# Causal attention with the normalisation on ScalarE, one root step, a single-precision projection, and the experts' loop written out

## The chip, the cores and the metric

The kernel runs on one core of a Trainium2 chip. The metric is the device time of one execution in microseconds (us). The core has engines that run side by side and wait for each other through semaphores: TensorE (PE, with its weight loads as PEld), VectorE (DVE), ScalarE (ACT), GpSimd (POOL), and SyncE (SP), which issues transfers. Each engine works through its own list of instructions in order, so an instruction that waits holds up everything behind it on that engine.

## The reference, cut to what matters

The network has two layers on x of shape 32 x 128 x 128 (32 sequences of 128 tokens, 128 features). The change lies in the last sub-layer, where a causal attention is followed by a mixture of experts:

```python
ln1_out = _layernorm(hidden_states, ln1_weight, ln1_bias)      # input is itself a normalised x
qkv = jnp.einsum('sbh,oh->sbo', ln1_out, qkv_weight)           # 16 query heads, 4 key/value heads of 8
scores = jnp.einsum('sbhd,tbhd->bhst', q, k) * scale
scores = jnp.where(causal, scores, jnp.finfo(scores.dtype).min)
probs = jax.nn.softmax(scores, axis=-1)
attn = jnp.einsum('bhst,tbhd->sbhd', probs, v).reshape(S, B, H)
hidden_after_attn = hidden_states + jnp.einsum('sbh,oh->sbo', attn, proj_weight)
ln2_out = _layernorm(hidden_after_attn, ln2_weight, ln2_bias)
gate = softmax(router logits); top 2 of 8 experts weigh gelu(ln2_out @ w1) @ w2
return hidden_after_attn + moe_out
```

The sequence axis of this attention is the batch axis of x: 128 independent causal attentions over 32 positions each. The input of the attention is normalised twice in a row: once as x's layer norm (the hidden state that the residual adds to), and once more by `ln1`. With variance v the first root is (v + eps)^-1/2. The second one acts on values whose variance is v / (v + eps), and the two together come to (v(1 + eps) + eps^2)^-1/2.

## The kernel before

The program has four parts one after the other: `layer0` and `attention1` (not touched), `attention2` (causal attention, about 561 to 744 us) and `experts1` (744 to 978 us).

`attention2` handles the 128 attentions as 32 steps ("quads") of 4, and 4 quads make a chunk: chunk n covers quads 4n to 4n + 3, and there are 8 chunks. Each engine runs a Python-unrolled function `step(q)` with n, k = q // 4, q % 4. Nothing but the order of these functions and their semaphores sets the order of the work. Around quad q:

- PE (`step` at L1425): transposes the row maxima of quad q (L1429), computes scores K.Q into bank TB (L1432, after the exponential of quad q - 1 has read it), then the scores Q.K of quad q + 1 into bank SB (L1441, L1443). SB also held the transposed maxima, so L1441 waits until ScalarE has copied them (`mT_ready`, the tile `mc`, L1216). Then come products of the next chunk's projections (`slot`: two at k = 0, two at k = 1, one at k = 2; lines 95 to 97), `widen` at k = 1 (L1422), `turn` at k = 3 (L1375, which transposes the normalised input of chunk n + 2), the subtraction of the maxima (L1455), the values (L1398) and the weighted sums of quad q - 1 (L1406, L1411).
- ACT (`step` at L1211): `mc` of quad q (L1216), the `slot` copies (L1201), at k = 1 and 2 two spreads of K (L1208), the exponential of quad q (L1226), at k = 0 a copy of the sums (L1231), and at k = 3 the copy of the transposed input (`high`, L1195) and the high half of the attention's output (L1236, f16 tile AT[0]).
- DVE (`step` at L1303): the maxima of quad q + 1 (L1307 to L1313), the `slot` rests (L1295, L1299), the masked values (L1320), at k = 1 `normalise(n + 2)` (L1281, four instructions of 128x128) and Af (L1344), at k = 2 the statistics (L1269, L1274), at k = 3 the low half of the transposed input (L1287) and the low half of the attention's output (L1347, f16 tile AT[1]).
- POOL (`step` at L1151): at k = 0 the sum Xq + Yq of chunk n + 3 (L1157), at k = 2 `prep(n + 3)`, a chain of seven dependent small instructions with two powers (L1137 to L1143), at k = 3 `hidden(n + 3)` (L1147).

Before quad 0 the same functions run the first chunks in from q = -12.

`experts1` goes over 8 groups of 4 sequences, 16 half-experts p per group. Per p, PE computes three f16 products of 128x512 (lines 95 to 97 with `w1`) and four f32 products of 128x128 (L1734, each recorded as two). At p = 0 it also computes the attention's projection of the next group as four split products of three f16 matmuls each (L1703, recorded at lines 95 to 97 as wp,AT), at p = 6 it transposes and at p = 9 it computes the router's logits. `over_groups` writes the steps for g = -1, 0 and 7 out and runs g = 1 to 6 in a hardware loop whose semaphore targets are computed in registers.

Of the kernel before, what the change touches and what calls it, by code (L numbers as in the profile page):

```python
# [12 lines left out]
F16 = mybir.dt.float16  # L13
# [7 lines left out]
G = B // GB  # L21
# [996 lines left out]
def attention2(nc, d, bank, keep, H, AT, wp):  # L1018
# [9 lines left out]
    with ExitStack() as ctx:  # L1028
# [10 lines left out]
        half = sb("half2", [128, 4])  # L1039
# [12 lines left out]
        rs = [sb(f"rs2_{i}", [128, 6, 4]) for i in range(2)]  # L1052
# [16 lines left out]
            s_psum s_max m_hi m_lo mT_psum mT_ready t_psum p_ready v_psum v_ready pv_done o_sb dd_inv dd_hi dd_lo r_psum at_f at_hi at_lo""")  # L1069
# [17 lines left out]
        with nc.Block() as block:  # L1087
            @block.gpsimd
            def _(pool):
# [40 lines left out]
                def prep(n):  # L1130
                    r, v = rs[n % 2], mv[n % 2][:, :, 1]

                    def link(ins, i):
                        ins.then_inc(s["root"], 1)
                        pool.wait_ge(s["root"], 7 * n + i)
                    pool.wait_ge(s["mv_ready"], n + 1)
                    link(pool.tensor_scalar(r[:, 0, :], v, 1.0, LN_EPS, ALU.mult, ALU.add), 1)  # L1137
                    link(pool.tensor_tensor(r[:, 1, :], r[:, 0, :], half[:], ALU.pow), 2)
                    link(pool.tensor_tensor(r[:, 2, :], r[:, 1, :], r[:, 1, :], ALU.mult), 3)
                    link(pool.tensor_tensor(r[:, 2, :], r[:, 2, :], v, ALU.mult), 4)  # L1140
                    link(pool.tensor_scalar(r[:, 3, :], r[:, 2, :], 1.0, LN_EPS, ALU.mult, ALU.add), 5)
                    link(pool.tensor_tensor(r[:, 4, :], r[:, 3, :], half[:], ALU.pow), 6)
                    link(pool.tensor_tensor(r[:, 5, :], r[:, 4, :], r[:, 1, :], ALU.mult), 7)  # L1143

                def hidden(n):
                    for k in range(4):
                        last = pool.tensor_scalar(H[:, 4 * n + k, :], Xq[:, 4 * n + k, :], mv[n % 2][:, k, 0:1],  # L1147
                                                  rs[n % 2][:, 1, k:k + 1], ALU.subtract, ALU.mult)
                    last.then_inc(s["h_ready"], 1)
# [17 lines left out]
            def _(act):  # L1167
# [18 lines left out]
                act.activation(wp[0][:], bank[1][:, 0:128], ACT.Copy).then_inc(s["hi"], 1)  # L1186
# [4 lines left out]
                act.wait_ge(s["zeros"], 1)  # L1191

# [18 lines left out]
                def step(q):  # L1211
# [16 lines left out]
                    if k == 0 and chunk(n - 1):  # L1228
                        act.wait_ge(s["pv_done"], q)
                        after(act, s["at_f"], n - 1)  # L1230
                        act.activation(Of[:], O[:], ACT.Copy).then_inc(s["o_sb"], 1)  # L1231
                    if k == 3 and chunk(n + 2):
                        high(n + 2)
                    if k == 3 and chunk(n - 1):
                        act.wait_ge(s["at_f"], n)
                        act.activation(tok(AT[0], n - 1), Af[:], ACT.Identity, bias=bv[:]).then_inc(s["at_hi"], 1)  # L1236
# [4 lines left out]
            def _(dve):  # L1241
# [4 lines left out]
                dve.tensor_tensor(wp[1][:], bank[1][:, 0:128], wp[0][:], ALU.subtract)  # L1246
# [29 lines left out]

                def normalise(n):
                    dve.wait_ge(s["root"], 7 * (n + 1))
                    after(dve, s["xT_psum"], n)
                    for k in range(4):  # L1280
                        last = dve.tensor_scalar(xn[:, k, :], Xq[:, 4 * n + k, :], mv[n % 2][:, k, 0:1],  # L1281
                                                 rs[n % 2][:, 5, k:k + 1], ALU.subtract, ALU.mult)
                    last.then_inc(s["xn_ready"], 1)
# [19 lines left out]
                def step(q):  # L1303
# [21 lines left out]
                    if k == 1 and chunk(n + 2):  # L1325
                        normalise(n + 2)
# [13 lines left out]
                    if k == 1 and chunk(n - 1):  # L1340
                        dve.wait_ge(s["r_psum"], n)
                        dve.wait_ge(s["o_sb"], n)
                        after(dve, s["at_lo"], n - 1)
# [129 lines left out]
def experts1(nc, d, bank, keep, X3, H, AT, wp, out):  # L1473
# [5 lines left out]
    with ExitStack() as ctx:  # L1479
# [43 lines left out]
        with nc.Block() as block:  # L1523
# [12 lines left out]
            def _(pool):  # L1536
# [17 lines left out]
                over_groups(pool, step, -1, G - 1)  # L1554

            @block.scalar
            def _(act):
# [26 lines left out]
                over_groups(act, step, -1, G - 1)  # L1584

            @block.vector
            def _(dve):
# [98 lines left out]
                over_groups(dve, step, -1, G - 1)  # L1686
# [4 lines left out]
            def _(pe):  # L1691
# [58 lines left out]
                over_groups(pe, step, -1, G - 1)  # L1750
# [4 lines left out]
def build(nc, d, out):  # L1755
    with ExitStack() as ctx:
# [22 lines left out]
        AT = [room.sb(f"AT{i}", [C, S * B], F16) for i in range(2)]  # L1779
        wp = [room.sb(f"wp{i}", [C, C], F16) for i in range(2)]  # L1780
# [20 lines left out]
```

## Time and profile before

| | us |
|---|---|
| median of 3 runs | 976.86 (973.74 to 979.70) |
| the profiled execution | 979.73 |
| its span, first to last instruction | 978.0 |
| PE busy | 783.1 (80%) |
| DVE busy | 689.6 (71%) |
| ACT busy | 429.1 (44%) |
| POOL busy | 220.6 (23%) |

The profile is of one execution. 1.73 us of its time lie outside the span. Busy shares are averages over four parts with different limits, so below they are read by stretch. A timeline row reads: start, duration, engine, line, operation, output<-inputs, shapes, count, and in brackets how long the engine idled before it and what ended that.

### The profile page before, as it was taken

To read this page: it belongs to the slowest core of one execution; us is meant where nothing else is said; L and a number is where in the kernel's file an instruction comes from. 1 tells how busy PE (TensorE), PEld (TensorE's weight loads), DVE (VectorE), ACT (ScalarE), POOL (GpSimd) and SP (SyncE) were. 2 spreads that over 40 slices of the span, in tenths; PEclk is the share of its full clock that TensorE was granted. 3 is DMA by queue.
4 is the path that set the end of the run, shared out by engine and by line. 5 is a ranking of instruction groups with operands and counts; after the bars stand their busy time and mean duration, and the time that the engine had idled before them with its cause. 6 is when DMAs were issued, how large, how long until landed. Compare 5 with 4: busy or idle time off the path is not lost. (4 is left out here: it accounts for less than half of the span.)

```text
span 978.0 us, 28213 instructions
## 1 busy us (share of the span) xinstructions
PE 783.1 (80%) x10948; PEld 595.1 (61%) x10948; DVE 689.6 (71%) x1882; ACT 429.1 (44%) x848; POOL 220.6 (23%) x369
## 2 busy tenths in 40 slices
PE   2579888887338999999999716887875899999998
PEld 1345555554236777777777513655654688888886
DVE  4578888875547888888888537887753666666653
ACT  2122222221215666666666415665642455555553
POOL 4333333330430111111110086543200111111100
PEclk9568889999758999999999958999996899999999
DMA  3000000510100000010010000000000000000000
GB/s 91 20 19 20 19 19 11 128 27 11 22 7 18 27 26 27 26 27 27 26 27 27 18 0 2 5 4 4 4 4 2 1 12 11 11 11 11 9 11 14
DMA packets 31381, 19.20 MB, mean 20 GB/s; under 512 B 10590, under 2 KB 29740, under 8 KB 31276
## 3 DMA queue, kind: packets, MB, share of 16 engines
q1 hardware_dynamic: 28236, 16.73, 6.7%
q8 instruction: 76, 1.25, 0.5%
q10 hardware_dynamic: 3040, 0.98, 0.4%
q14 instruction: 29, 0.24, 0.1%
HBM read 7.22 MB, written 2.10 MB: 10 GB/s over the span
## 5 line engine op out<-in xcount | busy, mean ns | idle before, releaser
L1734 PEld LDWEIGHTS bank<-w2r,hme 128*128 128x128 f32 x1024 | 132.2, 191 | 16.3 <-ACT hme L1575 2.1
L1734 PE MATMUL bank<-w2r,hme 128*128 128x128 f32 x1024 | 135.6, 276 | 0.5 <-DVE Xq L1677 0.5
L1575 ACT ACTIVATE hme<-bank,b 128x512 f32<-128x512 f32 x128 | 86.4, 687 | 96.0 <-PE bank L97 95.9
L833 DVE TENSOR_SCALAR bank<-bank 128x512 f32<-128x512 f32 x128 | 88.9, 695 | 28.7 <-PE bank L904 28.7
L1677 DVE SCALAR_TENSOR_TENSOR Xq<-bank,wgte,Xq 128x128 f32 (+1 forms) x256 | 72.1, 344 | 51.1 <-PE bank L1734 38.1
L754 ACT ACTIVATE P<-bank 128x512 f32<-128x512 f32 x128 | 76.7, 599 | 66.6 <-PE bank L913 66.4
L841 DVE TENSOR_REDUCE mx<-bank 128x4 f32<-128x512 f32 x128 | 87.1, 681 | 2.1 <-PE bank L896 2.1
L350 ACT ACTIVATE sg<-bank 128x512 f32<-128x512 f32 x40 | 23.9, 597 | 127.8 <-PE bank L581 94.0
L913 PE MATMUL bank<-mT,negsel 128*128 128x128 f16 x512 | 50.1, 220 | 16.8 <-DVE bank L833 12.7
L896 PE MATMUL bank<-K,Q 128*128 128x128 f16 x512 | 51.1, 224 | 11.9 <-issue 6.5
L728 POOL TENSOR_TENSOR inv_sum<-inv_sum,dn 128x16 f32<-128x16 f32 x32 | 7.0, 220 | 230.4 <-DVE dn L872 230.4
L592 PE MATMUL bank<-w_raw,hm 128*128 128x128 f32 x320 | 48.3, 300 | 4.7 <-DVE X L506 4.7
L592 PEld LDWEIGHTS bank<-w_raw,hm 128*128 128x128 f32 x320 | 43.7, 209 | 10.7 <-issue 9.1
L904 PE MATMUL bank<-Q,K 128*128 128x128 f16 x512 | 50.2, 221 | 0.0
L896 PEld LDWEIGHTS bank<-K,Q 128*128 128x128 f16 x512 | 33.0, 99 | 26.2 <-issue 18.3
L95 PE MATMUL bank<-xTe,w 128*128 (+1 forms) x128 | 48.8, 381 | 0.0
L96 PE MATMUL bank<-xTe,w 128*128 (+1 forms) x128 | 48.8, 381 | 0.0
L97 PE MATMUL bank<-xTe,w 128*128 (+1 forms) x128 | 48.8, 381 | 0.0
L913 PEld LDWEIGHTS bank<-mT,negsel 128*128 128x128 f16 x512 | 31.9, 98 | 27.6 <-issue 16.1
L1201 ACT ACTIVATE hmd<-bank,b8m,low 128x512 f16<-128x512 f32 x40 | 29.7, 774 | 38.6 <-PE bank L97 38.6
L924 PE MATMUL bank<-P,V 128*32 128x128 f32 x1024 | 41.4, 279 | 0.1
L95 PE MATMUL bank<-xT,w 128*128 128x512 f16 (+1 forms) x80 | 35.0, 437 | 5.9 <-DVE hm L482 4.7
(387 smaller groups left out, 2076.0 us busy)
## 6 DMA issues: line engine op xcount, KB each, us to landing
K<-Kc SPq DMA_DIRECT2D x128, 32.0 KB, 1.8
X<-in_x SPq DMA_DIRECT2D x8, 256.0 KB, 2.9
Xq<-X SPq DMA_DIRECT2D x32, 64.0 KB
Yq<-Y SPq DMA_DIRECT2D x32, 64.0 KB
out_x<-Xq SPq DMA_DIRECT2D x32, 64.0 KB, 1.7
cload<-in_ctx SPq DMA_DIRECT2D x8, 192.0 KB, 2.6
w1r<-in_L_ffn_moe_w SPq DMA_DIRECT2D x1, 1024.0 KB
w_raw<-in_L_ffn_w_gate ACTq DMA_DIRECT2D x1, 256.0 KB, 3.3
```

What stands on the lines that cost most here:

```text
L95: pe.matmul(ps, lhs[0], rhs[0], start=start, stop=False, **kw)
L96: pe.matmul(ps, lhs[0], rhs[1], start=False, stop=False, **kw)
L592: last = pe.matmul(DN[:, cols], hm[:, p, cols], w_raw[:, 2, p, :], start=(p == 0 and i == 0), stop=(p == NBLK - 1), skip_group_check=True)
L754: act.activation(P[j][:], TB[j % 2][:], ACT.Exp, scale=SCALE).then_inc(s["p_ready"], 1)
L833: dve.tensor_scalar(TB[j % 2][:], TB[j % 2][:], -CLIP, CLIP, ALU.max, ALU.min).then_inc(s["t_clip"], 1)
L841: dve.tensor_reduce(mx[:, 4 * j:4 * j + 4], SB[j % 2][:].rearrange("p (h k) -> p h k", h=4), AX.X, ALU.max).then_inc(s["s_max"], 1)
L896: last = pe.matmul(SB[j % 2][:, cols(h)], Q[b % RING][:, cols(h)], K[b % KR][j][:, cols(h)], start=True, stop=True)
L904: last = pe.matmul(TB[j % 2][:, cols(h)], K[b % KR][j][:, cols(h)], Q[b % RING][:, cols(h)], start=(h == 0), stop=False, skip_group_check= ...
L913: last = pe.matmul(TB[j % 2][:, cols(h)], negsel[:, 4 * j + h, :], mT[:], start=False, stop=True, skip_group_check=True)
L1575: act.activation(hm[:, p % HR], UP[p % RING][:], ACT.Gelu_apprx_tanh, bias=b1[:, p:p + 1]).then_inc(s["gelu"], 1)
L1677: last = dve.scalar_tensor_tensor(x, Y[e % 2][:, 128 * i:128 * i + 128], w, x, ALU.mult, ALU.add)
L1734: last = pe.matmul(Y[e % 2][:, cols], hm[:, p % HR, cols], w2r[:, p], start=(p % 2 == 0 and i == 0), stop=(p % 2 == 1), skip_group_check=True)
```

## The change

1. The second normalisation (`normalise`, four 128x128 instructions per chunk) goes from DVE to ACT, at the same k = 1, behind the exponential. It is now x * root + (-mean * root), so POOL also makes -mean * root (tile `ms`).
2. POOL's `prep` takes both roots in one power over 128x8: five instructions in place of seven, three of them dependent on one another in turn. It now also waits until an older chunk was normalised.
3. The attention's output AT is one f32 tile in place of a high and a low f16 tile: DVE's L1347 goes, ACT's L1236 stays and moves from k = 3 to k = 2. The projection weights `wp` are one f32 tile. The projection is four f32 matmuls per group in place of twelve f16 ones.
4. The four loops of `experts1` are written out in Python.

```diff
 def prep(n):                                  # POOL
     pool.wait_ge(s["mv_ready"], n + 1)
-    link(pool.tensor_scalar(r[:, 0, :], v, 1.0, LN_EPS, ALU.mult, ALU.add), 1)
-    link(pool.tensor_tensor(r[:, 1, :], r[:, 0, :], half[:], ALU.pow), 2)
...
-    link(pool.tensor_tensor(r[:, 4, :], r[:, 3, :], half[:], ALU.pow), 6)
-    link(pool.tensor_tensor(r[:, 5, :], r[:, 4, :], r[:, 1, :], ALU.mult), 7)
+    after(pool, s["xn_ready"], n - 1)
+    pool.tensor_scalar(ms[n % 2][:, 0, :], mv[n % 2][:, :, 0], -1.0, None, ALU.mult)
+    pool.tensor_scalar(r[:, 0, 0, :], v, 1.0, LN_EPS, ALU.mult, ALU.add)
+    pool.tensor_scalar(r[:, 0, 1, :], v, 1.0 + LN_EPS, LN_EPS * LN_EPS, ALU.mult, ALU.add
+                       ).then_inc(s["root"], 1)
+    pool.wait_ge(s["root"], 3 * n + 1)
+    pool.tensor_tensor(r[:, 1], r[:, 0], half[:], ALU.pow).then_inc(s["root"], 1)
+    pool.wait_ge(s["root"], 3 * n + 2)
+    pool.tensor_tensor(ms[n % 2][:, 1, :], ms[n % 2][:, 0, :], r[:, 1, 1, :], ALU.mult
+                       ).then_inc(s["root"], 1)
...
+def normalise(n):                             # now ACT
+    act.wait_ge(s["root"], 3 * (n + 1))
+    after(act, s["xT_psum"], n)
+    for k in range(4):
+        last = act.activation(xn[:, k, :], Xq[:, 4 * n + k, :], ACT.Identity, bias=ms[n % 2][:, 1, k:k + 1],
+                              scale=rs[n % 2][:, 1, 1, k:k + 1])
+    last.then_inc(s["xn_ready"], 1)
...
 # ACT, step(q), behind the exponential
+                    if k == 1 and chunk(n + 2):
+                        normalise(n + 2)
                     if k == 3 and chunk(n + 2):
                         high(n + 2)
-                    if k == 3 and chunk(n - 1):
+                    if k == 2 and chunk(n - 1):
                         act.wait_ge(s["at_f"], n)
-                        act.activation(tok(AT[0], n - 1), Af[:], ACT.Identity, bias=bv[:]).then_inc(s["at_hi"], 1)
+                        act.activation(tok(AT, n - 1), Af[:], ACT.Identity, bias=bv[:]).then_inc(s["at_done"], 1)
...
 # DVE, step(q)
-                    if k == 1 and chunk(n + 2):
-                        normalise(n + 2)
...
-                    if k == 3 and chunk(n - 1):
-                        dve.wait_ge(s["at_hi"], n)
-                        dve.scalar_tensor_tensor(tok(AT[1], n - 1), Af[:], bv[:], tok(AT[0], n - 1),
-                                                 ALU.add, ALU.subtract).then_inc(s["at_lo"], 1)
...
 # PE, experts1, p == 0
-                            last = split_product(pe, PX[:, 128 * i:128 * i + 128], [tok(t, g, 128 * i, 128) for t in AT],
-                                                 [w[:] for w in wp])
+                            last = pe.matmul(PX[:, 128 * i:128 * i + 128], tok(AT, g, 128 * i, 128), wp[:],
+                                             start=True, stop=True)
...
-                over_groups(pe, step, -1, G - 1)
+                for g in range(-1, G):
+                    step(g)
```

One chunk of ScalarE's list in `attention2`, before, from the exponential of k = 1 on (Pd is the exponential's output, mc the copied maxima, hmd a slot, Kd a spread, xTd the transposed input, Of the sums, AT the attention's output):

```order
L1226 ACTIVATE Pd<-bank 128x512
L1216 ACTIVATE mc<-bank 32x128
L1201 ACTIVATE hmd<-bank,b8m,low 128x512
L1208 ACTIVATE Kd<-Kc 32x16x32 x2
L1226 ACTIVATE Pd<-bank 128x512
L1216 ACTIVATE mc<-bank 32x128
L1226 ACTIVATE Pd<-bank 128x512
L1195 ACTIVATE xTd<-bank 128x512
L1236 ACTIVATE AT<-Af,bvd 128x512
L1216 ACTIVATE mc<-bank 32x128
```

The same place in the changed kernel:

```order
L1234 ACTIVATE Pd<-bank 128x512
L1197 ACTIVATE xn<-Xq,ms_1,rs_1 128x128 x4
L1224 ACTIVATE mc<-bank 32x128
L1209 ACTIVATE hmd<-bank,b8m,low 128x512
L1216 ACTIVATE Kd<-Kc 32x16x32 x2
L1234 ACTIVATE Pd<-bank 128x512
L1246 ACTIVATE AT<-Af,bvd 128x512
L1224 ACTIVATE mc<-bank 32x128
L1234 ACTIVATE Pd<-bank 128x512
L1203 ACTIVATE xTd<-bank 128x512
L1224 ACTIVATE mc<-bank 32x128
```

Four instructions now stand between the exponential of k = 1 and the copied maxima of k = 2, and AT stands ahead of the copied maxima of k = 3 where it stood ahead of those of the next k = 0.

TensorE's list in `experts1` around p = 0, where the projection stands between two products with the experts' weights, before (wp are the projection weights, w the experts'):

```order
L97 MATMUL bank<-xTe,w_1 128x512
L95 MATMUL bank<-wp,AT 128x128
L96 MATMUL bank<-wp,AT 128x128
L97 MATMUL bank<-wp,AT 128x128
L95 MATMUL bank<-wp,AT 128x128
L96 MATMUL bank<-wp,AT 128x128
```

The same place in the changed kernel:

```order
L97 MATMUL bank<-xTe,w_1 128x512
L1702 MATMUL bank<-wp,AT 128x128 x4
L95 MATMUL bank<-xTe,w_0 128x512
L96 MATMUL bank<-xTe,w_0 128x512
L97 MATMUL bank<-xTe,w_1 128x512
```

Twelve f16 matmuls (five are shown) gave way to four f32 ones. Nothing else moved in TensorE's list.

## Rows read from the trace of the kernel before

**Rows 1.** Stretches: length, then PE, PEld, DVE, ACT, POOL busy (count), clock, DMA, GB/s.
```profile
599.50:744.00 144.50, 110.64 (x4236) 80.15 (x4236) 104.00 (x276) 80.10 (x149) 43.83 (x70) 0.97 0.02 4
744.00:776.00 32.00, 22.77 (x143) 18.67 (x144) 17.46 (x52) 10.33 (x17) 5.39 (x9) 0.66 0.00 1
776.00:970.00 194.00, 194.00 (x1500) 159.51 (x1499) 118.97 (x423) 103.40 (x147) 14.70 (x18) 1.00 0.04 10
```

**Rows 2.** What PE waited for, 598 to 740 us: total, times, longest.
```profile
PE bank L1411 <- issue: 11.4, 10, 2.0
PE bank L1432 <- ACT Pd L1226: 8.8, 12, 1.3
PE bank L1441 <- ACT mc L1216: 6.6, 15, 0.7
...
PE bank L1429 <- DVE m L1313: 0.4, 1, 0.4
```

**Rows 3.** Timeline of ACT, from k = 1 to the next k = 0.
```profile
624.82 0.60 ACT L1226 ACTIVATE Pd<-bank 128x512 f32<-128x512 f32 x1
625.31 0.25 ACT L1216 ACTIVATE mc<-bank 32x128 bf16<-32x128 bf16 x1
...
629.10 0.60 ACT L1226 ACTIVATE Pd<-bank 128x512 f32<-128x512 f32 x1
629.59 0.25 ACT L1216 ACTIVATE mc<-bank 32x128 bf16<-32x128 bf16 x1
...
632.39 0.72 ACT L1236 ACTIVATE AT<-Af,bvd 128x512 f16<-128x512 f32 x1
633.02 0.25 ACT L1216 ACTIVATE mc<-bank 32x128 bf16<-32x128 bf16 x1
```

**Rows 4.** Timeline of PE in the same chunk.
```profile
632.29 0.23 PE L1429 MATMUL bank<-identb,m 128*128 128x128 bf16 x1
...
633.42 0.38 PE L1441 MATMUL bank<-Kd,Qd 128*128 128x128 f16 x4 [0.67 <-ACT mc L1216]
```

**Rows 5.** Groups of ACT: busy us, mean ns of one, idle before.
```profile
L1178 ACT ACTIVATE w8f<-wT 128x32 f32<-128x32 f32 x12 | 1.7, 214 | 2.8 <-POOL identb L1101 2.8
...
L1562 ACT ACTIVATE lnbr<-ones,ln_b 128x128 f32<-128x128 f32 x1 | 0.4, 386 | 0.0
...
L1184 ACT ACTIVATE wvd<-wvr,ln_w 128x32 f16<-128x32 f32 x1 | 0.3, 305 | 0.0
```

**Rows 6.** Groups of DVE that the change takes from it.
```profile
L1281 DVE TENSOR_SCALAR xn<-Xq,mv,rs 128x128 f32<-128x128 f32 x32 | 9.5, 364 | 3.4 <-POOL rs L1143 3.4
...
L1347 DVE SCALAR_TENSOR_TENSOR AT<-Af,bvd,AT 128x512 f16<-128x512 f32 x8 | 6.0, 752 | 2.6 <-ACT AT L1236 2.6
```

**Rows 7.** Groups of POOL: a power over 8 and over 4, a small product.
```profile
L279 POOL TENSOR_TENSOR rn<-n,half 128x8 f32<-128x8 f32 x8 | 13.9, 1733 | 32.2 <-DVE n L451 32.2
...
L1138 POOL TENSOR_TENSOR rs<-rs,half 128x4 f32<-128x4 f32 x8 | 8.3, 1033 | 0.7
...
L1139 POOL TENSOR_TENSOR rs<-rs 128x4 f32<-128x4 f32 x8 | 1.6, 198 | 0.6
```

**Rows 8.** Timeline of PE ahead of quad 0.
```profile
597.62 0.38 PE L1441 MATMUL bank<-Kd,Qd 128*128 128x128 f16 x4 [2.77 <-ACT Kd L1208]
```

**Rows 9.** The chain that ended last, start and length, around one p = 0.
```profile
813.69 0.89 PE bank L1734 x8
815.23 0.89 PE bank L1734 x8
817.43 0.95 PE bank L1734 x8
```

**Rows 10.** Timeline of PE at the experts' start.
```profile
753.25 0.27 PE L95 MATMUL bank<-wp,AT 128*128 128x128 f16 x1 [0.43 <-ACT rb L1566]
...
774.59 1.13 PE L1734 MATMUL bank<-w2r,hme 128*128 128x128 f32 x8 [0.47 <-DVE Xq L1677]
```

**Rows 11.** Loads of instructions, 776 to 816 us (queue, packets, MB, share).
```profile
q8 instruction: 3, 0.05, 0.6%
```

More of the change, by code:

```diff
@@ L1038, in attention2 @@
         selR = sb("selR", [128, 8, 128], F16)
-        half = sb("half2", [128, 4])
+        half = sb("half2", [128, 2, 4])
         pwp = sb("pwp", [C, 128])
@@ L1051, in attention2 @@
         mv = [sb(f"mv2_{i}", [128, 4, 2]) for i in range(2)]
-        rs = [sb(f"rs2_{i}", [128, 6, 4]) for i in range(2)]
+        rs = [sb(f"rs2_{i}", [128, 2, 2, 4]) for i in range(2)]
+        ms = [sb(f"ms2_{i}", [128, 2, 4]) for i in range(2)]
         xn = sb("xn2", [128, 4, C])
@@ L1068, in attention2 @@
             stats mv_ready root h_ready xn_ready xT_psum xT_hi xT_lo slot_psum slot_hi q_ready k_compact k_ready
-            s_psum s_max m_hi m_lo mT_psum mT_ready t_psum p_ready v_psum v_ready pv_done o_sb dd_inv dd_hi dd_lo r_psum at_f at_hi at_lo""")
+            s_psum s_max m_hi m_lo mT_psum mT_ready t_psum p_ready v_psum v_ready pv_done o_sb dd_inv dd_hi dd_lo r_psum at_f at_done""")
         PX, PJ, SB, TB, VM, O, D = bank[0], bank[1:3], bank[3], bank[4], bank[5], bank[6], bank[7]
@@ L1147, in hidden @@
                         last = pool.tensor_scalar(H[:, 4 * n + k, :], Xq[:, 4 * n + k, :], mv[n % 2][:, k, 0:1],
-                                                  rs[n % 2][:, 1, k:k + 1], ALU.subtract, ALU.mult)
+                                                  rs[n % 2][:, 1, 0, k:k + 1], ALU.subtract, ALU.mult)
                     last.then_inc(s["h_ready"], 1)
@@ L1185, in _ @@
                 act.wait_ge(s["pT"], 1)
-                act.activation(wp[0][:], bank[1][:, 0:128], ACT.Copy).then_inc(s["hi"], 1)
+                act.activation(wp[:], bank[1][:, 0:128], ACT.Copy).then_inc(s["hi"], 1)
                 act.wait_ge(s["bias"], 1)
@@ L1245, in _ @@
                 dve.wait_ge(s["hi"], 1)
-                dve.tensor_tensor(wp[1][:], bank[1][:, 0:128], wp[0][:], ALU.subtract)
                 dve.scalar_tensor_tensor(w8[1][:], w8f[:], lnw[:], w8[0][:], ALU.mult, ALU.subtract)
@@ L1275, in stats @@
                     last.then_inc(s["mv_ready"], 1)
[L1277 to L1283, printed above, removed]
                 def rest(n):
@@ L1342, in step @@
                         dve.wait_ge(s["o_sb"], n)
-                        after(dve, s["at_lo"], n - 1)
+                        after(dve, s["at_done"], n - 1)
                         dve.tensor_tensor(Af[:], Of[:], RB[:], ALU.mult).then_inc(s["at_f"], 1)
-                    if k == 3 and chunk(n - 1):
-                        dve.wait_ge(s["at_hi"], n)
-                        dve.scalar_tensor_tensor(tok(AT[1], n - 1), Af[:], bv[:], tok(AT[0], n - 1),
-                                                 ALU.add, ALU.subtract).then_inc(s["at_lo"], 1)
                 for q in range(FIRST, QUADS + 4):
@@ L1553, in step @@
                                                ).then_inc(s["r_ready"], 1)
-                over_groups(pool, step, -1, G - 1)
+                for g in range(-1, G):
+                    step(g)
             @block.scalar
@@ L1583, in step @@
                                            ACT.Exp).then_inc(s["g_exp"], 1)
-                over_groups(act, step, -1, G - 1)
+                for g in range(-1, G):
+                    step(g)
             @block.vector
@@ L1685, in step @@
                             prep(g + 1, p)
-                over_groups(dve, step, -1, G - 1)
+                for g in range(-1, G):
+                    step(g)
                 for e in (NE - 2, NE - 1):
@@ L1749, in step @@
                         down(late(g, p, LAG))
-                over_groups(pe, step, -1, G - 1)
+                for g in range(-1, G):
+                    step(g)
                 for p in range(NB - LAG, NB):
@@ L1778, in build @@
             attention1(nc, d, bank, keep, Y).end()
-        AT = [room.sb(f"AT{i}", [C, S * B], F16) for i in range(2)]
-        wp = [room.sb(f"wp{i}", [C, C], F16) for i in range(2)]
+        AT = room.sb("AT", [C, S * B])
+        wp = room.sb("wp", [C, C])
         attention2(nc, d, bank, keep, keep["X"], AT, wp)
```

6 lines of the change are left out of this document (removed).

## The prediction

> **What bounds the kernel now.** I began with busy time by stretch, because the causal attention (about 561 to 744 us) and the experts (744 to 978) have different limits. In the experts' steady part PE is busy for 194.00 of 194.00 us at full clock [rows 1]. There every instruction added to PE costs its full length, and whatever DVE or ACT do is free as long as it stays in their gaps. In the attention's steady part no engine is full: PE 110.64, DVE 104.00, ACT 80.10 and POOL 43.83 of 144.50 us [rows 1]. By these shares DVE, from which the change takes work, looks tighter than ACT, to which it gives work.
>
> The shares don't decide, the waits do. Second view: what PE waited for in that part [rows 2]. It waited for ACT 8.8 + 6.6 = 15.4 us in 27 places (the exponential ahead of L1432, the copied maxima `mc` ahead of L1441), and for DVE 0.4 us, once. Another 11.4 us are PE stopping inside L1411 without any semaphore. So the loop that sets a quad's length runs over ACT: `mc`, L1441, the slot products, their copy on ACT, the spreads, the exponential, then the next `mc`.
>
> Third view: the timeline of ACT around the two places where work is inserted. At k = 1 the exponential starts at 624.82 and `mc` of k = 2 at 625.31, while the exponential is still draining. At k = 2 the exponential starts at 629.10 and the next `mc` at 629.59 [rows 3]. There is no gap in either. The same holds in all six chunks that are normalised inside the steady part, and in five of the six that write AT there in mid-stream; in the sixth `mc` waits a quarter of a us for PE. At the third place, k = 3 to the next k = 0, AT stands ahead of `mc`, and there PE sometimes comes last anyway.
>
> **Part 1, normalise on ACT.** The trace of before has no ACT instruction of this exact kind (128x128 from SBUF, a pointer for the scale and one for the bias). Nearest is L1562, 386 ns for 128x128 with one pointer. A pointer costs 305 - 214 = 91 ns (L1184 against L1178, both 128x32) [rows 5]. With two that is 0.477 us, and neighbours on ACT overlap by 624.82 + 0.60 - 625.31 = 0.11 us [rows 3], so one step is 0.37 and four are 1.5 us. Ends: 4 x 0.28 = 1.1 if the second pointer is free, 4 x 0.477 = 1.9 without overlap. I take 1.5, since it is built from the nearest row.
>
> Queued behind them on ACT is `mc` of k = 2, and PE waits for it at L1441 (the bank of the scores also holds the maxima). Everything behind L1441 on PE moves with it, and so do the slot copies, the spreads and the exponential on ACT, which wait for those products. Nothing gives the time back within the quad. Six times in the steady part: + 9.0 us. A seventh time ahead of quad 0: PE waits there 2.77 us for ACT's spreads [rows 8], which now stand behind four more instructions: + 1.5. The first chunk's normalisation is followed by a long wait for POOL and costs nothing.
>
> What leaves DVE (9.5 us of busy time [rows 6], six of eight chunks in the steady part) I cost at nothing: PE waited for DVE only 0.4 us. The next late thing stays ACT.
>
> **Part 2, AT from k = 3 to k = 2.** AT takes 0.72 us, a step of 0.72 - 0.11 = 0.61. At k = 2 it stands ahead of a `mc` that had no gap [rows 3]: 6 x 0.61 = + 3.7 us. (The last chunk's AT falls where ACT waits for PE anyway.) At k = 3 it goes. There `mc` started at 633.02, behind AT at 632.39, though PE had its transposed maxima at 632.29 + 0.23 = 632.52, and PE waited 0.67 for it [rows 3, 4]. That gives back 0.5 us in the three chunks that look like this. In the other three `mc` waited for PE: in all - 1.4. DVE's L1347 (752 ns) goes [rows 6]. It counts only at the very end, where it is the last instruction before the experts may begin: - 0.75.
>
> **Part 3, POOL's roots.** Before: five small instructions at 0.2, two powers at 1.03 and gaps of 0.09 (0.7 over 8) make about 3.6 us. After: four small ones, one power over eight columns at 1.73 and two gaps, 2.7 us [rows 7]. In the steady part POOL idles two thirds of the time. Only the first chunk's chain is on the path, since the second chunk's sum, and DVE's work behind it, queue behind it on POOL: - 0.9. The new wait of `prep` is for a normalisation that was over long before.
>
> **Part 4, the projection in f32.** Four f32 matmuls of 128x128 are exactly one block of L1734: 0.89 us. The twelve f16 ones cost (817.43 - 815.23) - (815.23 - 813.69) = 0.66 us [rows 9]. So + 0.23 for each of six groups inside the full part, + 1.4. The first projection (753.25) lies on a serial chain in a stretch whose mean clock is 0.66 [rows 1, 10], so twice that, + 0.45. The second is followed by a wait of 0.47 us for DVE [rows 10], which swallows it: 0. Sum + 1.8. The bound from below is 0, if weight loading overlaps better than in L1734, from above 8 x 0.45 = 3.6, if all ran at the half clock.
>
> **Part 5, the loop written out.** PE has no gap over the whole 194 us [rows 1], six passes of the loop with their branches and registers among them. There is nothing to win: 0. It could lose through loads of instructions (a rival below).
>
> **Sum.** 9.0 + 1.5 + 3.7 - 1.4 - 0.75 - 0.9 + 1.8 = + 13.0 us. The profiled execution took 979.73 us (978.0 of span and 1.73 around it), so it would be 992.7. It was 2.9 us above the median of its runs. Carried to the median, 976.86 + 13.0 = 989.9 us.
>
> **Rivals.**
>
> (a) The stops inside L1411 absorb part of it. PE stopped there ten times, 11.4 us in all, 1.1 on average [rows 2]. The stop comes at a place that drifts slowly from quad to quad, and loads of instructions run in that stretch, so I read it as PE running dry of instructions. If the load is started ahead of the place where PE now waits longer, the wait hides the stop. Five of the twelve delayed quads have one: 2 x 1.1 + 3 x 0.6 = 4.0 us back, + 9.0, 985.9 us. Against it: where I can place them, loads start behind L1441.
>
> (b) DVE sets the pace, being busier than ACT (104.00 against 80.10 [rows 1]), and ACT has room for the rest. Then the attention gives up what leaves DVE: 6/8 x 9.5 + 7/8 x 6.0 = 12.4 us [rows 6], and 0.9 on POOL, against + 1.8 in the experts: - 11.5, 965.4 us. It decides as soon as PE's waits hang on the maxima or the slot rests of DVE. The 0.4 us of [rows 2] speak against it. The Trainium skill (Perfetto Trace Analysis, "Optimizing Scalar/DVE Operations") says that "if DVE is saturated, offloading some work to Scalar may make sense". The trace has DVE at 72% of the steady part, so by its own condition the rule doesn't apply here. The same section also warns of engines that aren't saturated and still cause bubbles elsewhere, which is what ACT does in [rows 2].
>
> (c) ACT hides both insertions, because the chain around them has slack that I don't see. Then - 1.4 - 0.75 - 0.9 + 1.8 = - 1.2 us, 975.6. Against it: in [rows 3] `mc` starts inside the exponential.
>
> (d) The written-out experts make PE run dry. Three loads fell into 40 us there [rows 11], about half of which is the loop's first pass; about 130 of the 194 us are later passes that now load too, some ten loads. At 1.1 us each, + 11 on top: 1000.9. Against it: those three loads happened while PE had no gap [rows 1]. PE's work there is in long matmuls, so a load has far more time.
>
> **How the numbers follow.** The forecast has 0.62, (a) 0.20, (b) 0.05, (c) 0.08, (d) 0.05. A measurement of this kernel tells about 0.5% (4.9 us) from no change. The forecast, (a) and (d) are slower by more than that (0.87), (c) is within it (0.08), (b) faster (0.05). The forecast's own range comes from the ends of the normalisation (7 x 0.4 both ways) and of the projection: 985 to 995. The clock may add a little, since PE idles more. To hold 8 in 10 the range goes down to 980, through (a) and the space below it, and up to 997. It leaves out (b), (c) and (d), 0.18.
>
> **What would show it.** In the changed profile ACT's normalisation has steps near 0.37 us and stands between exponential and `mc`. PE's wait at L1441 for `mc` (6.6 us before) grows to about 19, its wait for DVE stays under 1, and the steady attention grows from 144.5 to about 156 us. The projection reads 0.89 us per group, and a group of the experts is 0.23 us longer without a gap on PE. It is wrong if `mc` of k = 2 does not start later against PE's L1429 than before, if the stops inside L1411 shrink by more than a us or two (then (a)), or if PE shows idle time in the experts (then (d)).

## The result and the profile after

The changed kernel takes 993.62 us (median of 4 runs, 990.04 to 996.89), the kernel before 977.67 us in the same session (4 runs, 973.74 to 979.70). The ratio on record is 1.0143, with a 95% interval of 1.0103 to 1.0183: slower by 1.4%, or 14.0 us on 977.67. (The two medians by themselves are 16.0 us apart, and the runs of either kernel spread over 6 to 7 us.) Forecast were +13.0 us and 989.9 us. The profiled execution of the changed kernel took 996.89 us, its span 995.1 against 978.0 before.

Where the 17.1 us of span came in, read from the starts of the same instructions in the two timelines:

| stage | forecast | measured |
|---|---|---|
| up to the start of the last instruction of `attention1`, ahead of the change | 0 | 559.41 → 560.37: +1.0 |
| from there to the transposition of quad 0 (PE, L1429, now L1424) | +1.5 - 0.9 = +0.6 | 599.54 → 601.73: +1.2 |
| transpositions of quad 0 to quad 31 | +9.0 + 3.7 - 1.4 = +11.3 | 135.73 → 149.35: +13.6 |
| from there to the experts' first PE instruction | -0.75 | 9.00 → 8.09: -0.9 |
| experts | +1.8 | +2.2 |

The profile's page of the changed kernel: busy time, clock by slice (the last row) and loads of instructions.

```profile
PE 796.7 (80%) x10916; PEld 604.8 (61%) x10916; DVE 677.1 (68%) x1841; ACT 442.9 (45%) x880; POOL 215.7 (22%) x353
...
PEclk9978988889659999999999758999897799999999
...
q8 instruction: 84, 1.38, 0.6%
```

DVE lost 12.5 us of busy time, and the program got longer. The same stretches as in [rows 1], placed by the same instructions:

```profile
601.70:759.00 157.30, 115.97 (x4249) 83.69 (x4236) 94.02 (x244) 90.43 (x174) 38.68 (x56) 0.92 0.02 4
792.00:986.00 194.00, 194.00 (x1468) 160.00 (x1467) 119.30 (x421) 102.90 (x146) 14.76 (x18) 1.00 0.04 11
```

The causal attention takes 12.8 us more, with DVE emptier and ACT fuller. PE is busy 5 us longer for the same work, at a granted clock of 0.92 against 0.97. The experts still keep PE busy for 194.00 of 194.00 us.

What PE waited for, 598 to 755 us (total, times, longest), against [rows 2]:

```profile
PE bank L1436 <- ACT mc L1224: 14.1, 19, 1.5
PE bank L1406 <- issue: 11.1, 9, 1.9
PE bank L1427 <- ACT Pd L1234: 9.5, 13, 1.3
PE bank L1436 <- ACT Kd L1216: 4.1, 1, 4.1
PE bank L1436 <- issue: 3.3, 6, 0.6
```

L1436 is the old L1441. Its wait for `mc` went from 6.6 to 14.1 us, its longest from 0.7 to 1.5. Another 3.3 us stand at the same line under "issue", where the profile names no releaser. The timelines below show that these six are waits for `mc` too, so the wait for `mc` is 17.4 us in all. The stops in the weighted sums (L1406, the old L1411) are 11.1 against 11.4, and no row names DVE. The 4.1 us for Kd lie ahead of quad 0.

ACT in the changed kernel, from k = 1 to the `mc` of k = 3 ([rows 3] show such a chunk before; the columns are start and duration):

```profile
626.03 1.45 ACT L1209 ACTIVATE hmd<-bank,b8m,low 128x512 f16<-128x512 f32 x2 [1.43 <-PE bank L97]
...
628.67 0.60 ACT L1234 ACTIVATE Pd<-bank 128x512 f32<-128x512 f32 x1
629.30 1.65 ACT L1197 ACTIVATE xn<-Xq,ms,rs 128x128 f32<-128x128 f32 x4
630.85 0.25 ACT L1224 ACTIVATE mc<-bank 32x128 bf16<-32x128 bf16 x1
632.53 0.78 ACT L1209 ACTIVATE hmd<-bank,b8m,low 128x512 f16<-128x512 f32 x1 [1.43 <-PE bank L97]
...
634.64 0.60 ACT L1234 ACTIVATE Pd<-bank 128x512 f32<-128x512 f32 x1
635.26 0.72 ACT L1246 ACTIVATE AT<-Af,bvd 128x512 f32<-128x512 f32 x1
635.89 0.25 ACT L1224 ACTIVATE mc<-bank 32x128 bf16<-32x128 bf16 x1
```

PE in the same place:

```profile
628.68 0.23 PE L1424 MATMUL bank<-identb,m 128*128 128x128 bf16 x1
...
631.25 0.38 PE L1436 MATMUL bank<-Kd,Qd 128*128 128x128 f16 x4 [1.53 <-ACT mc L1224]
...
636.24 0.38 PE L1436 MATMUL bank<-Kd,Qd 128*128 128x128 f16 x4 [0.55 <-issue]
```

`mc` starts 2.18 us after the exponential where it started 0.49 us after it in [rows 3], and PE stands for 1.53 us with its maxima long transposed. The rows of the slots show the other side: behind `mc`, at k = 1 and at k = 2, ACT idles 1.43 us for PE's products, which stand behind L1436. The normalisation went into a spot without a gap, while one of 1.43 us opens right behind `mc`.

The last row is one of the six under "issue". Each of them is 0.55 us long, and in all six PE starts 0.10 us after the end of the `mc` that stood behind AT (here `mc` runs from 635.89 to 636.14). They are what AT's place at k = 2 costs: six times 0.55 us, where the forecast had six times 0.61.

### The profile page after: what moved, and what is told of

The parts are those of the page before. It is cut to its first block and busy times, and to the rows that moved or that the text cites. A ratio compares the mean times of both kernels' runs of the same rounds, so it can differ in the third digit from the quotient of the medians.

```text
span 995.1 us, 27244 instructions
## 1 busy us (share of the span) xinstructions
PE 796.7 (80%) x10916; PEld 604.8 (61%) x10916; DVE 677.1 (68%) x1841; ACT 442.9 (45%) x880; POOL 215.7 (22%) x353
## 5 line engine op out<-in xcount | busy, mean ns | idle before, releaser
L1674 DVE SCALAR_TENSOR_TENSOR Xq<-bank,wgte,Xq 128x128 f32<-128x128 f32 x256 | 72.1, 345 | 46.5 <-PE bank L1732 45.7
L592 PE MATMUL bank<-w_raw,hm 128*128 128x128 f32 x320 | 50.3, 308 | 4.5 <-DVE X L506 4.5
L592 PEld LDWEIGHTS bank<-w_raw,hm 128*128 128x128 f32 x320 | 46.3, 218 | 11.7 <-issue 10.0
L96 PE MATMUL bank<-xTe,w 128*128 128x512 f16 x128 | 49.3, 385 | 0.0
L95 PE MATMUL bank<-xTe,w 128*128 128x512 f16 x128 | 49.2, 385 | 0.0
L97 PE MATMUL bank<-xTe,w 128*128 128x512 f16 x128 | 49.2, 384 | 0.0
L1308 DVE TENSOR_REDUCE mxd<-bank 128x16 f32<-128x512 f32 x32 | 22.1, 690 | 27.1 <-PE bank L1438 26.9
```

What stands on the lines that cost most here:

```text
L95: pe.matmul(ps, lhs[0], rhs[0], start=start, stop=False, **kw)
L96: pe.matmul(ps, lhs[0], rhs[1], start=False, stop=False, **kw)
L97: return pe.matmul(ps, lhs[1], rhs[0], start=False, stop=stop, **kw)
L592: last = pe.matmul(DN[:, cols], hm[:, p, cols], w_raw[:, 2, p, :], start=(p == 0 and i == 0), stop=(p == NBLK - 1), skip_group_check=True)
L1674: last = dve.scalar_tensor_tensor(x, Y[e % 2][:, 128 * i:128 * i + 128], w, x, ALU.mult, ALU.add)
```

## The experiments

Line numbers are those of each kernel. Each set was timed beside the kernel before. Its medians there were 978.56, 980.38, 977.86 and 977.01 us, so the ratios are what is compared, and a difference in us with a sign is worked out from the ratio.

### The parts one at a time

**x_loop**, the experts' loops written out in the kernel before, nothing else:

```diff
-                over_groups(pe, step, -1, G - 1)
+                for g in range(-1, G):
+                    step(g)
```

> The kernel before with the experts' loops written out and nothing else. Theory A (ScalarE's place between exponential and copied maxima sets the loss; the loop is free because TensorE has no gap): within 1 us of the kernel before, experts' groups of 26.2 us, no idle time on TensorE. Rival D (written-out code makes TensorE run dry of instructions): + 5 to + 11 us, seen as idle time by issue in the experts' part.

Measured: 978.92 us, ratio 0.9983 (0.9955 to 1.0011). No price, no gain. The page counts 84 loads of instructions on q8 where the kernel before has 76, and PE stays full (194.00 of 194.00 us from 770 to 964). Rival (d) falls.

**x_proj**, the kernel before with AT and `wp` as single f32 tiles, AT left at k = 3, DVE's low half gone, loops written out:

```diff
-    act.activation(tok(AT[0], n - 1), Af[:], ...).then_inc(s["at_hi"], 1)        # k == 3
+    act.activation(tok(AT, n - 1), Af[:], ...).then_inc(s["at_done"], 1)         # k == 3
-    dve.scalar_tensor_tensor(tok(AT[1], n - 1), Af[:], ...)
-    split_product(pe, PX[...], [tok(t, g, 128 * i, 128) for t in AT], [w[:] for w in wp])
+    pe.matmul(PX[...], tok(AT, g, 128 * i, 128), wp[:], start=True, stop=True)
...
```

> [...] Theory A: + 1.8 in the experts (0.23 for each group, twice that for the first), - 0.75 at the attention's end, so + 1 us against the kernel before; the steady attention unchanged within 1 us. Rival B (VectorE sets the attention's pace): 7/8 x 6.0 = 5 us less in the steady attention, so - 4 us in all.

Measured: 979.12 us, ratio 0.9999 (0.9978 to 1.0020). What the forecast's terms for these parts come to (+1.8 - 0.75) lies inside that, and the 4 us less of rival (b) don't.

**x_norm**, the kernel before with only the normalisation on ACT behind the exponential of k = 1, and the one-step roots that feed it (`prep` and the body of `normalise` as in the change, not shown again):

```diff
 # ACT, step(q), behind the exponential
+                    if k == 1 and chunk(n + 2):
+                        normalise(n + 2)
 # DVE, step(q)
-                    if k == 1 and chunk(n + 2):
-                        normalise(n + 2)
```

> The kernel before with the normalisation on ScalarE behind the exponential of k = 1 and one power for both roots on GpSimd; AT, projection and loops as before. Theory A: 6 x 1.55 in the steady attention plus 0.6 ahead of quad 0, + 10 us, TensorE's wait for the copied maxima up by 8 or more. Clock share: a few half-clock stretches of 3.4 us more may add 1 to 3 us. Rival B (VectorE sets the pace): - 7 us. Rival C (ScalarE hides it): - 0.9 us.

Measured: 991.46 us, ratio 1.0116 (1.0085 to 1.0147), +11.3 us. PE's waits, 598 to 755 us:

```profile
PE bank L1441 <- ACT mc L1224: 15.8, 21, 1.5
PE bank L1411 <- issue: 11.2, 10, 1.7
PE bank L1432 <- ACT Pd L1234: 8.0, 12, 1.3
```

This part alone makes four fifths of the result, and it does so in the row that the prediction named. The terms for it were 9.0 + 1.5 - 0.9 = +9.6.

**y_norm_dve**, the reverse: the changed kernel with the normalisation back on DVE.

```diff
+                def normalise(n):                      # on DVE again
+                    dve.wait_ge(s["root"], 3 * (n + 1))
+                        last = dve.tensor_scalar(xn[:, k, :], Xq[:, 4 * n + k, :], mv[n % 2][:, k, 0:1],
+                                                 rs[n % 2][:, 1, 1, k:k + 1], ALU.subtract, ALU.mult)
...
+                    if k == 1 and chunk(n + 2):        # DVE, step(q)
+                        normalise(n + 2)
```

> The changed kernel with the normalisation back on VectorE (GpSimd's one-step roots, f32 projection, AT at k = 2 and written-out loops stay). Theory A: the normalisation's 9.4 and 1.5 go, 10 to 12 us faster than the changed kernel, 982 us. If VectorE's relief paid for part of the change, the loss would be given back: less than 8 us faster.

Measured: 983.23 us, ratio 1.0025 (1.0004 to 1.0045), +2.5 us. That is what the forecast has left without the normalisation: 3.7 - 1.4 - 0.75 - 0.9 + 1.8 = +2.5.

### Place or load

**z_dve_twice**, the kernel before, DVE normalising twice, once into a tile that nobody reads:

```diff
+                    for k in range(4):
+                        dve.tensor_scalar(spare[n % 2][:, k, :], Xq[:, 4 * n + k, :], mv[n % 2][:, k, 0:1],
+                                          rs[n % 2][:, 5, k:k + 1], ALU.subtract, ALU.mult)
```

> The kernel before with the normalisation done twice on VectorE, the first time into a tile that nobody reads, so VectorE carries 1.1 to 1.2 us more per chunk. Theory A (VectorE has slack in the attention): within 2 us of the kernel before. Rival B (VectorE sets the pace): + 7 to + 9 us.

Measured: 980.47 us, ratio 1.0020 (0.9993 to 1.0047). PE's waits, 598 to 740 us:

```profile
PE bank L1436 <- ACT Pd L1227: 7.7, 12, 1.3
PE bank L1445 <- ACT mc L1217: 6.8, 15, 0.7
PE bank L1433 <- DVE m L1317: 2.0, 4, 0.7
```

Four normalisations more per chunk cost 2.0 us on DVE (the interval reaches from -0.7 to 4.6, below the 7 to 9 that rival (b) asks for) and 11 us on ACT at the changed kernel's place. DVE had the room, and rival (b) falls.

**y_norm_early**, the changed kernel with `normalise` moved within ACT's k = 1 from behind the exponential to behind `mc`, ahead of the slot copies:

```diff
                         act.activation(mc[0:32, :], ...).then_inc(s["mT_ready"], 1)
+                    if k == 1 and chunk(n + 2):
+                        normalise(n + 2)
                     if chunk(n + 1):
                         for i in ((0, 1), (2, 3), (4,), ())[k]:
                             slot(n + 1, i)
...
```

> The changed kernel with ScalarE's normalisation moved within its quad: directly behind the copied maxima of k = 1, ahead of the slot copies, where ScalarE waits 1.43 us for TensorE in the trace, instead of behind the exponential. Same work on every engine. Theory A (place, not load): 9 to 11 us faster than the changed kernel, 983 us, + 5 against the kernel before (AT's 0.6 x 6 stays); the wait at L1436 for the copied maxima of k = 2 gone. Rival E (ScalarE's added load itself costs, through its rate or its busy time): within 2 us of the changed kernel, 993 us.

Measured: 981.56 us, ratio 1.0020 (0.9996 to 1.0044). The +2.0 us lie below the +5 that was expected (the interval ends at +4.3) and near the +2.5 that the prediction's other terms come to. ACT at that place:

```profile
615.83 0.25 ACT L1224 ACTIVATE mc<-bank 32x128 bf16<-32x128 bf16 x1
615.99 1.63 ACT L1197 ACTIVATE xn<-Xq,ms,rs 128x128 f32<-128x128 f32 x4
617.53 1.43 ACT L1209 ACTIVATE hmd<-bank,b8m,low 128x512 f16<-128x512 f32 x2
618.85 1.27 ACT L1216 ACTIVATE Kd<-Kc 32x512 f16<-32x512 f16 x2
620.14 0.60 ACT L1236 ACTIVATE Pd<-bank 128x512 f32<-128x512 f32 x1
620.64 0.25 ACT L1224 ACTIVATE mc<-bank 32x128 bf16<-32x128 bf16 x1
```

The same four instructions, of the same 1.6 us, on the same engine, in the same step. They fill the time in which ACT waits for PE's products, and `mc` of the next quad again starts 0.50 us behind its exponential. Twelve us come back by moving them past five instructions of one step. The price was the place, not the engine's load. The cost of AT's place is still in this kernel: its profile has five more waits of 0.55 us under "issue" at L1436.

**y_both_early**, AT of k = 2 moved there as well:

```diff
+                    if k == 2 and chunk(n - 1):
+                        act.wait_ge(s["at_f"], n)
+                        act.activation(tok(AT, n - 1), Af[:], ...).then_inc(s["at_done"], 1)
                     if chunk(n + 1):
                         for i in ((0, 1), (2, 3), (4,), ())[k]:
                             slot(n + 1, i)
...
```

> As y_norm_early, and AT of k = 2 also directly behind the copied maxima. Theory A: a further 3 to 4 us faster, 979 to 980 us, + 1 to 2 against the kernel before. Rival E: 993 us.

Measured: 979.64 us, ratio 1.0001 (0.9977 to 1.0024): the whole change in other places costs nothing that can be measured. The waits of 0.55 us are gone from its profile.

### What AT's place costs

**y_at3**, the changed kernel with AT put back to k = 3:

```diff
-                    if k == 2 and chunk(n - 1):
+                    if k == 3 and chunk(n - 1):
                         act.wait_ge(s["at_f"], n)
```

> The changed kernel with AT put back to k = 3 on ScalarE. Theory A: - 3.7 for k = 2 and + 1.4 for k = 3, so 2.3 us faster than the changed kernel, 991 us. If AT's place doesn't matter: 993.6 us.

Measured: 994.49 us, ratio 1.0142 (1.0107 to 1.0177), against 1.0143 of the changed kernel. The gain of 2.3 us isn't there. Its profile shows where it went (598 to 755 us):

```profile
PE bank L1436 <- ACT mc L1224: 15.6, 21, 1.5
```

The six waits under "issue" are gone, and all waits for `mc` are 15.6 us against 17.4: 1.8 less, near the forecast. But the stops of PE in the weighted sums are 12.3 us against 11.1, and the execution spent 29.3 us between quads 0 and 31 at half the clock against 22.0. Together these can hide 2 us, and four runs of each can't decide. So I enlarged the term.

**w_at_k2_twice** and **w_at_k3_twice**, the kernel before with two extra copies of AT's kind at either place:

```diff
+                    if k == 2 and chunk(n - 1):                 # the other kernel: k == 3
+                        act.wait_ge(s["at_f"], n)
+                        act.activation(spare[0][:], Af[:], ACT.Identity, bias=bv[:])
+                        act.activation(spare[1][:], Af[:], ACT.Identity, bias=bv[:])
                     if k == 3 and chunk(n + 2):
                         high(n + 2)
```

> The kernel before, with two extra copies of AT's kind (128x512, single precision to f16, into spare tiles that nobody reads) at k = 2 behind the exponential, where the change puts AT. Two steps of 0.61 us are 1.22 us per chunk. Theory A (what stands between the exponential and mc on ScalarE pushes the whole chain by its full length): six chunks in mid-stream and the end, 7 x 1.22 = +8.5 us, about 986.4 us where the kernel before takes 977.9. Theory B, from the kernel with AT put back to k = 3, which won nothing: the price of this place is about half of that or less, because the stops for instructions and the clock take part of it: +4 us or less, about 982.

> The same two extra copies at k = 3, behind the exponential and ahead of the transposed input and AT, as the kernel before orders them. Theory A: in three chunks AT already makes mc late and they cost in full, in three mc waited for PE by some tenths of a us: 3 x 1.22 + 3 x 0.8 and 1.22 at the end, +7.3 us, about 985.2, so 1 to 2 us less than at k = 2. If k = 3 were a free place for AT, as the gain of 2.3 us claimed for putting it there supposes at the most, it would be under +4. Theory B (no difference of place that can be measured): the same as at k = 2 within 1 us.

Measured: at k = 2 987.7 us, ratio 1.0099 (1.0063 to 1.0135), +9.7 us; at k = 3 984.79 us, ratio 1.0071 (1.0045 to 1.0097), +6.9 us. Both are where theory A had them (+8.5 and +7.3). At k = 2 the interval starts at 6.2 us, above the +4 that theory B allowed, and at k = 3 at 4.4 us, above the +4 that a free place would have cost. At k = 2 the profile again has six waits at the same product under "issue", 7.0 us in all for two copies. If one copy costs half of two, it is 4.8 against 3.5 us. AT's move is then worth some +1.4 us where the forecast had +2.3; the intervals of the two overlap, so that they differ at all is likely, not shown. That two copies on ACT cost several us at either place is shown.

### Two that missed: making the list better than it was

If ACT's work behind `mc` is free, the kernel before should gain from it too. **z_spread_early** moves its spreads of K there:

```diff
+                    if k in (1, 2) and chunk(n + 1):
+                        spread(n + 1, 2 * k - 2)
+                        spread(n + 1, 2 * k - 1)
                     if chunk(n + 1):
                         for i in ((0, 1), (2, 3), (4,), ())[k]:
                             slot(n + 1, i)
-                    if k in (1, 2) and chunk(n + 1):
-                        spread(n + 1, 2 * k - 2)
-                        spread(n + 1, 2 * k - 1)
```

> The kernel before with ScalarE's two spreads of k = 1 and of k = 2 moved directly behind the copied maxima, ahead of the slot copies, so they no longer stand between those and the exponential. Same work. Theory A: the exponential of k = 1 and 2 starts up to 1.27 us sooner, TensorE's 8.8 us of waits for it nearly vanish: 7 to 10 us faster than the kernel before, 969 us. If the stops inside TensorE's L1411 take the time back: 3 to 5 us faster.

Measured: 978.96 us, ratio 1.0000 (0.9972 to 1.0029), which also excludes the 3 to 5 us that were expected if the stops took part of the gain. PE's waits, 598 to 740 us:

```profile
PE bank L1411 <- issue: 11.2, 10, 1.9
PE bank L1441 <- ACT mc L1216: 7.1, 23, 0.5
PE bank L1398 <- issue: 3.0, 5, 1.1
PE bank L1441 <- DVE Qd L1299: 2.7, 3, 2.0
PE bank L1406 <- issue: 1.8, 2, 1.5
PE bank L1429 <- issue: 1.2, 1, 1.2
...
PE bank L1432 <- ACT Pd L1226: 0.2, 1, 0.2
```

The wait for the exponential went as expected, from 8.8 us to 0.2. Others took its place: the stops without a releaser sum to 17.9 us over five rows (14.2 before), DVE's Qd and small ones to 3.6 (0.4), `mc` 7.1 (6.6). All of PE's waits together are 28.8 us against 30.0. This profile also has 12.6 us at half the clock between quads 0 and 31 against 6.0, so not all of the missing gain need be the stops.

**z_all_early**, the changed kernel with all of ACT's side work behind `mc`: the normalisation at k = 0, the spreads at k = 1 and 2, AT at k = 3.

```diff
+                    if k == 0 and chunk(n + 2):
+                        normalise(n + 2)
+                    if k == 3 and chunk(n - 1):
+                        act.wait_ge(s["at_f"], n)
+                        act.activation(tok(AT, n - 1), Af[:], ...).then_inc(s["at_done"], 1)
+                    if k in (1, 2) and chunk(n + 1):
+                        spread(n + 1, 2 * k - 2)
+                        spread(n + 1, 2 * k - 1)
...                                             # the same lines go at their old places
```

> The changed kernel with all of ScalarE's side work directly behind the copied maxima: normalisation at k = 0, spreads at k = 1 and 2, AT at k = 3. Theory A: none of it stands between slot copies, exponential and the next copied maxima; like z_spread_early less 1 us of roots and end, plus 1.8 of the f32 projection: 966 to 971 us, which beats both kernels. Rival E: 985 us or more, since ScalarE's load is the changed kernel's.

Measured: 979.81 us, ratio 1.0028 (1.0000 to 1.0055). By the ratios it is 11 us below the changed kernel, and it isn't below the kernel before, where 966 to 971 us were expected. Its waits have the same shape:

```profile
PE bank L1406 <- issue: 12.6, 10, 1.9
PE bank L1436 <- ACT mc L1224: 6.7, 23, 0.6
PE bank L1393 <- issue: 3.0, 5, 0.8
PE bank L1401 <- issue: 2.6, 2, 1.5
```

The exponential's wait is 1.4 us, the rows under "issue" (two of 0.9 aren't shown) 20.0, and all waits together 29.8 us. No version that was run beats the kernel before by more than the noise.

## Why the prediction was right

**The mechanism.** That ACT's order and not DVE's load decides was read from the waits in [rows 2] and the missing gap in [rows 3]. x_norm put the price on ACT's place, z_dve_twice took it off DVE, and y_norm_early gave 12 us back with the load unchanged. Rival (c), no loss at all, lies outside the measured interval. The mark set beforehand was that `mc` of k = 2 starts later against PE's transposition. It does: 630.85 against 628.68 is 2.17 us behind it. Before, it was 0.48 us, from `mc` at 625.31 [rows 3] and this row:

```profile
624.83 0.23 PE L1429 MATMUL bank<-identb,m 128*128 128x128 bf16 x1
```

**The normalisation, +9.0 and +1.5.** Built from neighbours, a step was to be 0.37 us and one instruction 0.477. The changed kernel's row, where the columns after the bar are busy time and ns of one:

```profile
L1197 ACT ACTIVATE xn<-Xq,ms,rs 128x128 f32<-128x128 f32 x32 | 13.2, 485 | 11.0 <-POOL ms L1142 10.8
```

Four take 1.65 us, a step of (1.65 - 0.485) / 3 = 0.39. In the quads from k = 2 to k = 3 of the six chunks the changed kernel fell behind by 2.7, 1.7, 2.0, 1.5, 1.5 and 3.0 us, 12.4 in all for 9.0 forecast. x_norm has 11.9 in the same six quads, and none of the kernels with the normalisation elsewhere has more than 1.6. Four of them lie at 1.5 to 2.0. The first and the last are larger by a us, and both contain a stretch at half the clock (613.6 to 617.0 and 709.1 to 712.5, more below); so does one of the 1.5. Ahead of quad 0 the wait for the spreads grew from 2.77 [rows 8] to:

```profile
599.44 0.59 PE L1436 MATMUL bank<-Kd,Qd 128*128 128x128 f16 x4 [4.09 <-ACT Kd L1216]
```

That is +1.3 for a forecast of 1.5. The stage as a whole grew by 1.2 us where +0.6 was forecast. Of the rest, 0.4 us lie between this product and the transposition of quad 0, which takes 2.29 us against 1.92.

**Rival (a), the stops absorb part.** In the row that the prediction watched they didn't: 11.1 us against 11.4. With the neighbouring row (the old L1406, 2.8 us, which the changed kernel has no more) it is 11.1 against 14.2, 3.1 us less, where (a) had 4.0. x_norm has 14.0. One execution can't tell such a difference: x_loop, whose attention is that of the kernel before, has 10.3. As a whole (a) would have ended at 985.9 us, which the result excludes. That part of a later wait is hidden in this way isn't excluded.

**AT's move, +3.7 - 1.4.** What AT costs at k = 2 is read directly from the six waits of 0.55 us: 3.3 for 3.7 forecast. What leaving k = 3 gives back is the uncertain part. Read in the same way as above, the six steps from k = 3 to the next k = 0 that follow AT grew by 5.0 us, and the seven from k = 0 to k = 1 shrank by 2.7: +2.3 in all, but stretches at half the clock lie in both sums. By the enlarged runs the move is nearer +1.4, and y_at3 shows no gain from undoing it. Together with the projection and the rest, y_norm_dve has +2.5 us measured for +2.5 forecast, with an interval of 0.4 to 4.4 that holds both.

**Roots, -0.9.** In the changed kernel the first chain on POOL runs from 578.83 to the end of its last small product at 581.96, 3.1 us, where before it took from 577.70 to 581.57, 3.9 us: 0.7 less for 0.9 forecast. The power over eight columns takes 1670 ns:

```profile
L1140 POOL TENSOR_TENSOR rs<-rs,half 128x8 f32<-128x8 f32 x8 | 13.4, 1670 | 0.7
```

**The experts, +1.8.** The chain that ended last, around one p = 0 (start and length):

```profile
805.26 0.89 PE bank L1732 x8
806.79 0.89 PE bank L1702 x8
807.68 0.89 PE bank L1732 x8
```

The projection is one block of 0.89 us, as taken. The first one, in the stretch with the low clock, went from 1.46 to 2.06 us, +0.6 for 0.45. The stage grew by 2.2 for 1.8. Written out, the program loads eight more blocks of instructions and shows no gap.

**Where the size was off, and where luck helped.** 13.6 us came in between quads 0 and 31 for 11.3 forecast. PE's waits and its busy time in that stretch say what they are made of. The two stretches, from the transposition of quad 0 to that of quad 31, before and after:

```profile
599.54:735.27 135.73, 107.55 (x4083) 77.76 (x4084) 100.49 (x269) 77.31 (x144) 43.79 (x70) 0.98 0.02 4
601.73:751.08 149.35, 112.67 (x4092) 81.17 (x4083) 92.06 (x239) 88.22 (x170) 38.65 (x56) 0.93 0.02 4
```

PE waited 10.8 us more for `mc` (6.6 to 17.4) and 0.7 more for the exponential. That is 11.5 us for the 11.3 of the sum: the mechanism is right in size too. Two things that the sum didn't hold came on top. PE's busy time grew by 5.1 us for the same products, and its stops without a releaser shrank by some 3 us. They partly cancel, and that is luck: with the clock alone the result would have been some 3 us further off.

The 5.1 us go with the clock, which the prediction had mentioned ("the clock may add a little") and not sized. Two stretches of the changed kernel:

```profile
613.60:617.00 3.40, 3.06 (x120) 2.06 (x118) 2.12 (x7) 2.33 (x4) 0.00 (x0) 0.51 0.02 5
617.00:620.40 3.40, 2.99 (x134) 2.59 (x134) 2.38 (x13) 1.77 (x5) 2.04 (x4) 1.00 0.02 5
```

In the first the granted clock is at its lower level, 1.2 GHz, in the second at 2.4 GHz. By the clock's records in the traces, 22.0 us between quads 0 and 31 are at the lower level in the changed kernel and 6.0 in the kernel before. Over all fourteen profiled kernels, which do the same work on PE there, that time runs from 6.0 to 29.3 us and PE's busy time from 106.4 to 115.2, and a straight line through them has 0.34 us of busy time per us at the lower level (correlation 0.96). For 16.0 us more that is an estimate of 5.4 us, where 5.1 was measured.

That the longer waits for ACT bring the low clock on is likely and not shown. The three kernels with the normalisation ahead of `mc` have 15.5 us (x_norm), 22.0 (the changed kernel) and 29.3 (y_at3) at the lower level, the eleven others 6.0 to 17.2. In all three, and in none of the others, such a stretch lies in the k = 2 quads of the first and of the sixth chunk, which are the two that were a us too long above. But y_both_early has 17.2 us with a ratio of 1.0001, and no run changes the waits without moving the work.

## What to carry to other kernels

Before moving work to a less busy engine, look in its timeline for a gap at the very place where the work will stand, and ask who waits for the next instruction behind it. Here 1.6 us of work cost its full length each time ahead of the copy that TensorE waits for, and nothing that could be measured behind it. A wait that the profile puts under "issue" can still be one for another engine: look at what ended just before it. When a large wait of an engine is removed, count all of its waits before expecting the sum, since others may have been hidden under it.

## What was not expected of the hardware

**Stops of PE follow loads of instructions in a dense stretch of short matmuls.** PE's stops without a releaser end at a nearly fixed distance from loads on the queue q8. In the kernel before, one packet is listed in the window from 643.4 to 643.6 us (packets, MB, share of the queues' time):

```profile
q8 instruction: 1, 0.02, 29.5%
```

and PE resumes at:

```profile
645.92 0.25 PE L1411 MATMUL bank<-Pd,gmj 128*32 128x32 f32 x2 [0.95 <-issue]
```

Eight pairs (load to within 0.2 us, end of the stop) are 643.4 and 645.92, 647.8 and 650.08, 652.4 and 654.82 in the kernel before, 651.0 and 653.72 in the changed one, and 641.0 and 643.63, 645.4 and 647.83, 649.6 and 652.26, 666.4 and 669.14 in z_spread_early: 2.3 to 2.7 us each. In the whole attention of the kernel before, 12 of the 13 stops end 2.2 to 2.5 us after the start of a load, and the one that doesn't is of 0.2 us. From 625 to 655 us there are seven loads, about one per quad. The four ahead of these (627.8 to 639.0) have no stop in the list of waits. Within 3 us of each of them PE waited for ACT instead (1.30, 0.67, 0.50 and 0.25 us).

That fits what the two misses show: where a wait for ACT went, a stop came, and the waits together were 28.8 and 29.8 us of 142 against 30.0. It isn't a fixed sum, though: y_norm_early, with PE's list unchanged, has 32.3. No kernel was run with fewer or more instructions on PE, so that the loads cause the stops rests on this timing alone. In the experts, where PE's list is of long matmuls, the same kind of load came without a gap on PE. Whether a shorter instruction stream on TensorE would let the better order pay is open.
